# Masked weights applied through v's column totals, and all P transposed from moved words

## The reference

```
scores = jnp.einsum('bhfc,bhtc->bhft', k, q)          # 8 heads of 64
causal = jnp.triu(jnp.ones((s, s), dtype=bool))
scores = jnp.where(causal[None, None], scores, -10000.0)
attn = jax.nn.softmax(scores, axis=-2)
vals = jnp.einsum('bhft,bhfc->bhtc', attn, v)
```

## Time and profile before

| | |
|---|---|
| time, median of 3 | 1449.1 us |
| the profiled execution's own time | 1449.89 us |
| its span, first to last instruction | 1447.8 us |
| busy: TensorE, VectorE, ScalarE, GpSimd | 1430.7, 918.8, 692.6, 625.7 us |
| granted TensorE clock, mean | 0.999 of 2.4 GHz |

### The profile page before, as it was taken

One profiled execution on the slowest core, in us unless ns is written; L12 is line 12 of the kernel. 1 busy time (PEld: TensorE's weight loads), 2 busy tenths in 40 slices (PEclk: granted clock), 3 DMA queues, 4 the chain that ended last, 5 costly groups with the idle time before them and its releaser, 6 DMA issues.

```text
span 1447.8 us, 24821 instructions
## 1 busy us (share of the span) xinstructions
PE 1430.7 (99%) x7852; PEld 1272.1 (88%) x7852; DVE 918.8 (63%) x2118; ACT 692.6 (48%) x1497; POOL 625.7 (43%) x1154
## 2 busy tenths in 40 slices
PE   7999999999999999999999999999999999999998
PEld 6888888888888888888888889999999999999998
DVE  7576675675775775765755886555555555555554
ACT  6375465564573664754654863333333323333332
POOL 3353452461553453534523674444444334444442
PEclk9999999999999999999999999999999999999999
DMA  7333323223233223333223622222222222222211
GB/s 247 124 95 84 118 71 120 87 82 117 91 91 106 94 76 112 94 85 115 71 77 91 212 87 100 103 103 102 101 93 82 92 101 95 93 101 101 94 70 61
DMA packets 63636, 146.25 MB, mean 101 GB/s; under 512 B 6896, under 2 KB 28912, under 8 KB 63600
## 3 DMA queue, kind: packets, MB, share of 16 engines
q1 hardware_dynamic: 63600, 145.80, 30.7%
HBM read 60.06 MB, written 25.69 MB: 59 GB/s over the span
## 4 chain that ended last, share of the span: by engine, by line
PE 97%; DVE 1%; DMA 1%; ACT 0%; POOL 0%; issue 0%; DVEq 0%; POOLq 0%; SPq 0%
PE ps_f L2018 26%; PE ps_o L1382 20%; PE ps_o L1413 12%; PE ps_o L1970 11%; PE ps_s L1433 6%; PE ps_v L1260 4%; PE ps_o L1376 3%; PE ps_v L1261 3%; PE ps_t L1291 2%; PE ps_f L1999 2%; PE ps_t L1293 2%; PE ps_o L1336 2%; PE ps_o L1452 1%; PE ps_x L1989 1%; PE ps_t L1382 1%; PE ps_t L1269 1%
## 5 line engine op out<-in xcount | busy, mean ns | idle before, releaser
L2018 PE MATMUL ps_f<-wagh,x2Th 128*128 128x364 f32 x768 | 254.8, 332 | 1.1 <-DVE wagl L779 1.1
L2018 PE MATMUL ps_f<-wagh,x2Tl 128*128 128x364 f32 x768 | 252.6, 329 | 0.0
L2018 PE MATMUL ps_f<-wagl,x2Th 128*128 128x364 f32 x768 | 252.2, 328 | 0.0
L1382 PE MATMUL ps_o<-xTh,wh 128*128 128x512 f32 x424 | 173.5, 409 | 0.0
L1382 PE MATMUL ps_o<-xTh,wl 128*128 128x512 f32 x424 | 166.5, 393 | 0.0
L1382 PE MATMUL ps_o<-xTl,wh 128*128 128x512 f32 x424 | 165.6, 391 | 0.0
L2018 PEld LDWEIGHTS ps_f<-wagh,x2Th 128*128 128x128 f32 x768 | 144.2, 188 | 2.6 <-DVE wagl L779 1.4
L2018 PEld LDWEIGHTS ps_f<-wagl,x2Th 128*128 128x128 f32 x768 | 144.5, 188 | 1.1
L2018 PEld LDWEIGHTS ps_f<-wagh,x2Tl 128*128 128x128 f32 x768 | 144.4, 188 | 0.0
L541 POOL TENSOR_TENSOR cw<-wm,cnt 128x4 f32<-128x4 f32 x64 | 12.9, 201 | 296.9 <-ACT pr L1044 296.9
L564 POOL TENSOR_SCALAR pr<-pr,rden 128x512 f32<-128x512 f32 (+3 forms) x256 | 135.5, 547 | 0.0
(11 more groups left out here) (224 smaller groups left out, 3474.6 us busy)
## 6 DMA issues: line engine op xcount, KB each, us to landing
p_words<-pr SPq DMA_DIRECT2D x42, 448.0 KB, 2.7
kst<-kst SPq DMA_DIRECT2D x64, 256.0 KB, 3.7
xt<-in_x SPq DMA_DIRECT2D x32, 512.0 KB, 4.1
x2r<-x2n SPq DMA_DIRECT2D x30, 512.0 KB, 2.9
xs<-in_x SPq DMA_DIRECT2D x24, 512.0 KB, 4.5
out<-x SPq DMA_DIRECT2D x23, 512.0 KB, 3.0
valsT<-vt SPq DMA_DIRECT2D x64, 128.0 KB, 2.3
vraw<-valsT SPq DMA_DIRECT2D x32, 256.0 KB, 3.5
```

The source lines that it names most:

```text
L1382: done = pe.matmul(ps[:, :], w[:, k, c:c + P], xT[:, k, :], start=(k == 0 and w is wh and xT is xTh), stop=(k == KD - 1 and w is wl), skip ...
L2018: last = pe.matmul(ps_f[:, g, 0:GW], a[:, k, :], w[:, k, cols], start=(k == 0 and a is xh and w is wagh), stop=False, skip_group_check=True)
```

## The change

The masked weights are no longer spread over blocks beside P. Since w(t) is the same for all masked f, P minus w can be used inside the diagonal block and below, and w(t) times a total of v added once per row t:

- `denominator` also computes `nwm = -wm`; `normalise` does `(pr + nwm) * rden` in one instruction, after a drain. The high products in `values` then have 512, 384, 256, 128 columns like the low ones.
- Once a batch, ScalarE and VectorE add v's four tiles up in `vt` (a copy of tile 0, three additions), the sum is split (`vsum_hi`, `vsum_lo`), `value_totals` on TensorE multiplies it by ones (two matmuls of 512 columns into `ps_t[1]`), and `totals_hi`, `totals_lo` split the result. `vsum_lo` stands at the end of slot 1 on VectorE, ahead of `p_lo(0, 2)`, and `totals_lo` behind `scores_max(2)`; on ScalarE `vsum_hi` stands ahead of `p_hi(0, 2)`, and `totals_hi` opens slot 2, ahead of a copy of x and of `exps(2)`.
- `value_totals_spread` adds, for each head, `totals` times the diagonals (one matmul of 384 columns) into `ps_v` behind the head's products. `masked_weights` and `masked_spread` are gone; `diagonal` has two buffers and waits for `pv_done` of two heads before.
- All heads of the loop's batches are moved by `move_p`. The transposes g = 0, 1 of heads 0, 5 and 7 come half a projection later (slots 1, 6, 8); g = 2 of head 7 goes into the middle of slot 9's half. The evacuations `p_hi`, `p_lo` of head 7 move with them.

```diff
@@ sync
-                    if h in (7, 9):
-                        dup_k((h - 7) // 2, b + 1)
-                    if 2 <= h < 6 or h > 6:
+                    if h == 9:
+                        dup_k(1, b + 1)
+                    if 2 <= h < 6 or h > 7:
                         store_vals(h - 2, b)
-                    if h in MOVED:
+                    if h == 7:
+                        dup_k(0, b + 1)
+                        store_vals(h - 2, b)
+                    if h < NH:
                         move_p(h, b)
@@ gpsimd
                 pool.tensor_tensor(den[:, q, :], cw[:, q, :], acc[:, q, :], ALU.add).then_inc(den_ready, 1)
+                pool.tensor_tensor(nwm[:, q, :], wm[:, q, :], mone[:, :].to_broadcast([P, 4]), ALU.mult)
...
-                pool.wait_ge(wn_done, H + 1)
-
-                pool.wait_ge(wt_ready, 1 + H)
-                pool.tensor_tensor(W_DIAGONAL.rearrange("p (i t) -> p i t", i=3),
+                pool.wait_ge(pv_done, H + 1)
+                pool.tensor_tensor(DIAGONALS[q].rearrange("p (i t) -> p i t", i=3),
...
+                pool.drain()
                 for i in reversed(range(NT)):
                     at = pr[:, q, S_OFF[i]:S_OFF[i] + (i + 1) * P]
-                    done = pool.tensor_scalar(at, at, rden[:, q, i:i + 1], 1.0, ALU.mult, ALU.mult)
+                    done = pool.tensor_scalar(at, at, nwm[:, q, i:i + 1], rden[:, q, i:i + 1], ALU.add, ALU.mult)
@@ vector v_lo
                 dve.wait_ge(v_high, 4 * b + t + 1)
+                if t > 0:
+                    dve.wait_ge(v_low, 4 * b + t)
+                    done = dve.tensor_tensor(vt[:, :], ps_j[t % 2][:, :], vt[:, :], ALU.add)
+                    if t == NT - 1:
+                        done.then_inc(vsum_ready, 1)
...
+            def vsum_lo(b):
+                dve.wait_ge(vsum_high, b + 1)
+                dve.tensor_tensor(VSUM_LOW, vt[:, :].rearrange("p (h c) -> p h c", h=NH // 2), VSUM_HIGH.bitcast(F32),
+                                  ALU.subtract).then_inc(vsum_low, 1)
+
+            def totals_lo(b):
+                dve.wait_ge(totals_high, b + 1)
+                dve.tensor_tensor(totals[:, :, HD:2 * HD], ps_t[1][:, :].rearrange("p (h c) -> p h c", h=NH),
+                                  totals[:, :, 0:HD].bitcast(F32), ALU.subtract).then_inc(totals_low, 1)
...
@@ scalar
+            def vsum_hi(b):
+                act.wait_ge(vsum_ready, b + 1)
+                act.activation(VSUM_HIGH, vt[:, :].rearrange("p (h c) -> p h c", h=NH // 2), ACT.Copy)\
+                    .then_inc(vsum_high, 1)
+
+            def totals_hi(b):
+                act.wait_ge(totals_full, b + 1)
+                act.activation(totals[:, :, 0:HD], ps_t[1][:, :].rearrange("p (h c) -> p h c", h=NH), ACT.Copy)\
+                    .then_inc(totals_high, 1)
...
+                if t == 0:
+                    act.wait_ge(vals_stored, 16 + 16 * 8 * b)
+                    act.activation(vt[:, :], ps_j[0][:, :], ACT.Copy)
@@ scalar body
-                    if h >= 2:
-                        masked_spread(h - 2, b)
+                    if h == 2:
+                        totals_hi(b)
@@ tensor
             for j in range(NT):
-                pe.matmul(ps_v[:, :], v[:, j, h, :], HIGH_ROWS[j], start=(j == 0), stop=False, skip_group_check=True)
-                last = pe.matmul(ps_v[:, j * P:], v[:, j, h, :], LOW_ROWS[j], start=False, stop=(j == NT - 1),
-                                 skip_group_check=True)
-            last.then_inc(pv_done, 1)
+                for rows in (HIGH_ROWS[j], LOW_ROWS[j]):
+                    pe.matmul(ps_v[:, j * P:], v[:, j, h, :], rows, start=(j == 0 and rows is HIGH_ROWS[0]), stop=False,
+                              skip_group_check=True)
+            if h > 0:
+                value_totals_spread(pe, h, b)
+
+        def value_totals_spread(pe, h, b):
+            H = 8 * b + h
             pe.wait_ge(d_ready, H + 1)
-            pe.wait_ge(t_lo, 3 * H + 2)
-            pe.matmul(ps_t[1][:, 0:3 * P], ones[:, 0:1].to_broadcast([P, P]), W_DIAGONAL,
-                      start=True, stop=True).then_inc(t_full[1], 1)
+            pe.matmul(ps_v[:, 0:3 * P], totals[:, h, :], DIAGONALS[h % 2], start=False, stop=True,
+                      skip_group_check=True).then_inc(pv_done, 1)
+
+        def value_totals(pe, b):
+
+            pe.wait_ge(vsum_low, b + 1)
+            pe.wait_ge(t_lo, 3 * 8 * b + 2)
+            for part in (VSUM_HIGH, VSUM_LOW):
+                last = pe.matmul(ps_t[1][:, :], ones[:, 0:1].to_broadcast([P, P]), part.rearrange("p h c -> p (h c)"),
+                                 start=(part is VSUM_HIGH), stop=(part is VSUM_LOW))
+            last.then_inc(totals_full, 1)
...
-            elif g == 1:
-
-                pe.wait_ge(wt_ready, 1 + H)
-            else:
+            elif g == 1 and h == 1:
+                pe.wait_ge(totals_low, b + 1)
+            elif g == 2:
                 pe.wait_ge(t_lo, 3 * H + 1)
@@ tensor body
-                    steps(h, 0, b)
+                    if h == NH + 1:
+                        half_step(h, 0, 0, b)
+                        transpose_p(pe, NH - 1, 2, b, True)
+                        half_step(h, 0, 1, b)
+                    else:
+                        steps(h, 0, b)
...
+                    if h == 2:
+                        value_totals(pe, b)
                     if h >= 2:
                         values(pe, h - 2, b)
-                    if 1 <= h <= NH:
-                        transpose_p(pe, h - 1, 0, b, h - 1 in MOVED)
-                        transpose_p(pe, h - 1, 1, b, h - 1 in MOVED)
+                    if 1 <= h <= NH and h not in (1, BARE, NH):
+                        transpose_p(pe, h - 1, 0, b, True)
+                        transpose_p(pe, h - 1, 1, b, True)
+                    if h == 2:
+                        value_totals_spread(pe, 0, b)
                     turns(h, 1, b)
-                    steps(h, 1, b)
+                    if h == 1:
+                        half_step(h, 1, 0, b)
+                    else:
+                        steps(h, 1, b)
+                    if h in (1, BARE, NH):
+                        transpose_p(pe, h - 1, 0, b, True)
+                        transpose_p(pe, h - 1, 1, b, True)
+                    if h == 1:
+                        half_step(h, 1, 1, b)
```

More of the change, by code:

```diff
@@ L286, in attention_phase @@
         p_ready = sem("p_ready")
-        p_moved = sem("p_moved")
+        p_moved = [sem(f"p_moved{i}") for i in range(2)]
         ident_turned = sem("ident_turned")
@@ L862, in body @@
                         lows(h, 1, b)
-                    if 1 <= h <= NH and h not in (BARE, BARE + 1):
+                    if h == 1:
+                        vsum_lo(b)
+                    if h == NH:
+                        for g in range(2):
+                            p_lo(h - 1, g, b)
+                    if 1 <= h < NH and h not in (BARE, BARE + 1):
                         p_lo(h - 1, 2, b)
@@ L879, in last_body @@
                 v_lo(3, b)
+                vsum_lo(b)
                 p_lo(0, 2, b)
                 scores_max(2, b)
+                totals_lo(b)
                 vals_sum(0, b)
@@ L1127, in body @@
                         highs(h, 1, b)
-                    if 1 <= h <= NH and h not in (BARE, BARE + 1):
+                    if h == 1:
+                        vsum_hi(b)
+                    if h == NH:
+                        for g in range(2):
+                            p_hi(h - 1, g, b)
+                    if 1 <= h < NH and h not in (BARE, BARE + 1):
                         p_hi(h - 1, 2, b)
@@ L1152, in last_body @@
                 p_hi(1, 2, b)
-                masked_spread(1, b)
                 q_hi(2, b)
@@ L1474, in steps @@
                 items = between(BETWEEN_LAST if last else BETWEEN, h, part, b)
-                if part == 0 and h >= 2 and len(items) == 1:
-                    kind, p, row, ks = items[0]
-                    items = [(kind, p, row, ks[:len(ks) // 2]), (kind, p, row, ks[len(ks) // 2:])]
-                for n, (kind, p, row, ks) in enumerate(items):
+                for kind, p, row, ks in items:
                     step(kind, p, row, ks, last)
-                    if n == 0 and part == 0 and h >= 2:
-                        masked_weights(pe, h - 2, b)
             def turns(h, place, b):
@@ L1486, in turns, with half_step @@
                     transpose_x(t, g, b + 1)
+            def half_step(h, part, half, b):
+                (kind, p, row, ks), = between(BETWEEN, h, part, b)
+                step(kind, p, row, ks[len(ks) // 2 * half:len(ks) // 2 * (half + 1)], False)
             def body(b):
@@ L1505, in body @@
                         scores(h + 1, b)
-                    if 1 <= h <= NH:
-                        transpose_p(pe, h - 1, 2, b, h - 1 in MOVED)
+                    if 1 <= h < NH:
+                        transpose_p(pe, h - 1, 2, b, True)
             def last_body(b):
```

(8 more changed lines are left out.)

96 lines of the change are left out of this document (44 added, 52 removed).

## The result

The changed kernel takes 1452.39 us (median; 1450.16 to 1453.79), the kernel before 1449.38 beside it (1448.25 to 1450.16). The ratio is 1.0019, with an interval of 1.0013 to 1.0026: a little slower, where a faster kernel of 1443.2 was forecast. The profiled execution took 1452.51 us, its span is 1450.7, the mean granted clock 0.999.

A forecast was written before the change was run, and what follows sets the result against it. TensorE's program was taken as the bound, with chains through other engines close behind. Seven bodies at -0.70 us (-4.9) and the last at -1.0 gave -5.9: 1444.0 profiled, 1443.2 against the median; range 1435 to 1451.

The forecast's parts named there:

- TensorE's work: TensorE's matmuls and transposes: a loop body loses 2.40 us of work, 18.9 us in all if nothing became late.
- the fourth rival: TensorE's issue distance is set by weight load more than columns; 0.10 us saved a head, no change, 1450; 3%.
- Slots 1 and 2, the totals: Start of a body: TensorE waits 0.2 us for totals_lo at head 1's transposes and is +0.34 us late in sum.
- The second rival: The new totals decide: head 1's transposes wait up to 1.5 us behind totals_lo; slower, 1455.1 at that bound; 11%.
- Slots 2 to 4: Up to scores(4): a ScalarE and VectorE chain swallows the cuts; nothing gained, scores(4) late by the same +0.34 us.
- slot 4 to slot 5: To the end of q in slot 5: values(2), its spread and dropped masked_weights(3) gain 0.32 us, no wait near.
- Slots 5 to 8: To vals_sum(5)'s end: a chain limits the gain to 0.15 us of TensorE's 1.1; head 5's transfers stay covered.
- the third rival: Head 7's moved P lands late and the 0.57 us at the body's end is lost; 1447.2, no change; 17%.
- Slots 8, 9, 0: End of a body: values(6), masked_weights(7), head 7's transposes and values(7) gain 0.57 us; P fits by 0.3.
- The last body: Final body, where TensorE waits for VectorE at its end: half of 2.1 us gained, -1.0 (bounds 0 and -2.1).
- The first rival: The waits give way because chains shorten with TensorE; the whole 18.9 us goes, 1430.2; 15%.
- above 101.4 a body: a new wait: Sign of being wrong: a loop body above 101.4 us, where 100.7 was forecast, would mean a new wait.

The follow-up runs named there:

- e5: The changed kernel with GpSimd's division by one scalar as before, without drain, nwm and the masked weight's subtraction; 1447.67 us, ratio 0.9989.
- e11: The changed kernel with GpSimd's split of x's tile 1 in slot 5 put behind head 5's division; 1449.38 us, ratio 0.9999.
- e2: The kernel before with only the change's transfers of all heads and later transposes, without nwm and totals; 1458.5 us, ratio 1.0061.
- e7: The changed kernel with the high and low words of q's pair 0 earlier, ahead of head 7's reciprocal; 1451.22 us, ratio 1.001.
- e13: The changed kernel with e11's order and only ScalarE's half of e7 (q's high words earlier); 1445.94 us, ratio 0.9973.
- e3: The changed kernel with the moves undone: heads 5 and 7 read directly, all transposes at their old places; 1460.45 us, ratio 1.007.
- e1: The kernel before with only the high products narrowed to 512, 384, 256, 128 columns; 1441.85 us, ratio 0.9945.
- e16: The changed kernel with 60 empty drains ahead of TensorE's first transposes, to shift its instruction loads; 1451.34 us, ratio 1.0015.
- e14: e13 with 60 empty drains ahead of TensorE's first transposes, to shift its instruction loads; 1443.94 us, ratio 0.9962.
- e4: The changed kernel with GpSimd's diagonal(5) held until VectorE's last small step of scores_max(6) is done; 1452.94 us, ratio 1.0025.
- e12: The changed kernel with the orders of e7 and e11, and scores_max(6) ahead of a split of x on VectorE; 1447.72 us, ratio 0.9983.

## Why the prediction was wrong

- *TensorE's work.* Right in kind (the fourth rival, 0.10 a head, is out), too large: the narrow products save 0.27 instead of 0.32 a head at `values(3)`, and the spread keeps 0.23 of TensorE where I put 0.17. With both, 8 x (0.27 + 0.17 - 0.23) + 0.30 - 0.46 = 1.5 us a body in place of 2.40.
- *Slots 1 and 2, the totals: +0.34.* Right in kind: +0.16 up to `scores(3)`. `totals_lo` ended at 478.33, just where the second four of head 1's transposes start, and all eight took 0.72 instead of 0.67 us. The second rival fell.
- *Slots 2 to 4: nothing gained; slot 4 to slot 5: -0.32.* Right: +0.03, and -0.24.
- *Slots 5 to 8: -0.15, "its DMAs fit under that delay".* This step failed, by 0.42. The sum asked only whether the evacuation of head 5's transposes could wait; it never put the landing of its P beside TensorE's arrival, as it did for head 7. The late arrival was the third rival's mechanism at a head that this rival did not name. The second error fed it: "the drain and `nwm` add about 0.1" left out that the division itself takes 633 instead of 547 ns an instruction, in all some 0.5 us a head. e5 takes 0.4 out of this place, e11 0.56, and with e11 the stretch is -0.41: better than forecast. The reading "TensorE already arrives no later than its input" was also wrong for `values(6)`: at 535.59 it followed the matmul before it by 0.24, without a wait.
- *Slots 8, 9, 0: -0.57.* Failed, by 0.65. Head 7's P did land in time (542.37 for transposes at 543.12). But moving eight of its transposes behind half a projection brings this half forward, and its bank was still being read. The forecast followed the moved step and not what moved up into its place; e2 shows the price alone (+1.27), e7 and e13 take 0.4 to 0.5 out of the stretch. The wait of `values(6)` behind `vals_sum(5)`, 0.43 us, stays in every order tried on the change. The stretch that ends with it, from `scores(7)`, grew with the moves and not with the totals: 12.57 us before, 12.99 with the moves alone (e2), 12.45 with the totals alone (e3, where a wait of 0.2 stands too). Whether head 5's move or head 7's does it wasn't separated.
- *The last body: -1.0, taken as half of its shrunken work.* This failed too: it was -0.13. Up to `values(5)` it had gained 1.22 us; behind that it lost 1.09 again, 0.65 of it in the wait for `y`. With e5's edits the last body is 1.53 us shorter than before, and that wait is gone; so GpSimd's longer division, or what goes with it, takes most of it back. It isn't the whole cause: e1, with the division of before, waits 0.8 us for `y` as well.
- *Not in the sum:* the first body, +2.27 in the profile, perhaps 1 in the median (e16).
- *The first rival* (all waits give way, 18.9 us) did not come: the waits grew.

The bound of "above 101.4 a body: a new wait" was met, with several: two of them, at head 5's P and at q's bank, make the body slower than before. With these two mended and the load shifted, the kernel is 5.5 us below the one before (e14), where the forecast had 5.9. That the two are so near is partly luck: e14's body gives 0.8 where the forecast had 0.70, its last body 0.1 where it had 1.0.

## What to carry to other kernels

When a step on the bounding engine is moved back, do the sum for the step that moves forward into its place as well: which buffer or bank does it need, and who still holds it there. When an input is changed from a direct read to a transfer, write its landing time beside the arrival of its reader, for each instance and not for one. And when a kernel scatters more than the other, look in its first loop body and in its start for losses that come once, before explaining the scatter by its work.

## What the runs showed of the hardware

- GpSimd's `tensor_scalar` with two scalars per partition took 633 ns on the mean of four widths (the change), with one and a constant 547 (e5 and the kernel before).
- Loads of instructions run on the same DMA engines as the kernel's transfers. In five profiles one of 16 KB (0.9 to 1.4 us) fell into the 192 KB transfer of head 2's P, and this one took 4.5 to 5.6 us; in the other nine it did not, and the transfer took 2.4 to 2.7.
- 60 empty drains ahead of the loop moved that load by some 7 us (79.2 to 72.2 in the changed kernel). The median fell by 2.0 us in one kernel and by 1.1 in the other.
- A VectorE step of 128x3 took 0.90 us beside GpSimd's diagonal (the change) and 0.17 with the diagonal held back (e4).
- Behind TensorE's wait of 3.1 us in e3 the granted clock fell to the lower level for a time (0.66 on the mean of the next 5 us), and behind one of 2.7 in e12 too (0.50 from 86 to 88 us); behind 2.15 us in the change and 2.9 in e7 it stayed at 1.00.
